# Issuing the value weighings of two neighbouring key tiles together in a four-batch attention kernel

## What is computed

```python
qkv = (x @ Wqkv.T + bqkv).reshape(Bb, Ss, 3, H, HD).transpose(2, 0, 3, 1, 4)
q, k, v = (qkv[0], qkv[1], qkv[2])
attn = jax.nn.softmax(jnp.einsum('bhid,bhjd->bhij', q, k) / jnp.sqrt(jnp.float32(HD)), axis=-1)
...
mod = attn * coh[..., None]
mod = mod / (mod.sum(-1, keepdims=True) + 1e-08)
...
mod = (1.0 - fi) * mod + fi * fa[:, None, :, None]
out = jnp.einsum('bhij,bhjd->bhid', mod, v).transpose(0, 2, 1, 3).reshape(Bb, Ss, Ee)
return out @ Wout.T + bout
```

## Time and profile before

| | |
|---|---|
| three runs | 308.05, 307.35, 306.35 us (median 307.35) |
| profiled execution, span from the first to the last instruction | 302.4 us |
| TensorE (PE) busy | 272.4 us, 90% |
| VectorE (DVE) busy | 197.7 us, 65% |
| ScalarE (ACT) busy | 176.2 us, 58% |
| GpSimd (POOL) busy | 157.9 us, 52% |
| mean granted TensorE clock | 0.977 |

### The profile page before, as it was taken

How to read it: one execution, slowest core, us unless ns; L and a number is a source line. 1 busy time by engine, 2 the same in 40 slices (tenths; PEclk the granted TensorE clock), 3 DMA queues, 4 the chain that set the end, 5 groups by cost and what they waited for, 6 DMA issues and landing times.

```text
span 302.4 us, 4278 instructions
## 1 busy us (share of the span) xinstructions
PE 272.4 (90%) x1579; PEld 130.0 (43%) x1579; DVE 197.7 (65%) x227; ACT 176.2 (58%) x214; POOL 157.9 (52%) x143
## 2 busy tenths in 40 slices
PE   8999397598979999999899999999999988899973
PEld 6447244233534444444444454446444433344422
DVE  6485355556777677887577668785876778864113
ACT  3224034456667768676448677674667666655760
POOL 3933639998199999993003069960000399900000
PEclk9999687989999999999999999999999999999999
DMA  7717839739773934399318933695159500101002
GB/s 240 214 44 217 192 53 121 175 61 120 138 245 52 125 37 152 98 117 173 126 69 109 109 83 122 96 121 171 54 86 121 90 2 4 33 3 69 1 0 72
DMA packets 16020, 31.11 MB, mean 103 GB/s; under 512 B 2232, under 2 KB 8248, under 8 KB 14656
## 3 DMA queue, kind: packets, MB, share of 16 engines
q1 hardware_dynamic: 15168, 30.15, 50.9%
q10 hardware_dynamic: 832, 0.69, 0.8%
HBM read 20.21 MB, written 10.49 MB: 102 GB/s over the span
## 4 chain that ended last, share of the span: by engine, by line
PE 59%; DVE 18%; DMA 13%; issue 4%; SPq 2%; POOL 1%; ACT 1%; DVEq 0%; ACTq 0%; POOLq 0%
PE o_ps L1018 15%; DVE maxima L660 14%; PE job_ps L794 12%; PE pair_ps L990 11%; PE pair_ps L1003 9%; DMA stack<-qk_scratch 6%; PE job_ps L908 4%; DMA stack<-max_rows 3%; DVE qk_lo L676 2%; DMA w_raw<-wqkvT 2%; DMA qk_scratch<-qk_lo 2%; SPq L313 1%; PE pair_ps L882 1%; PE job_ps L849 1%; PE pair_ps L794 1%
## 5 line engine op out<-in xcount | busy, mean ns | idle before, releaser
L660 DVE TENSOR_REDUCE maxima<-pair_ps 128x2 f32<-128x1024 f32 x128 | 155.5, 1222 | 69.1 <-PE pair_ps L990 69.1
L513 ACT ACTIVATE probs<-pair_ps 128x1024 f32<-128x1024 f32 x128 | 130.8, 1025 | 65.6 <-PE pair_ps L1003 64.9
L990 PE MATMUL pair_ps<-stack 48*128 48x512 f32 x256 | 64.5, 500 | 8.2 <-DMA stack<-qk_scratch 7.6
L1018 PE MATMUL o_ps<-probs,vals 128*32 128x512 f32 x512 | 69.0, 612 | 0.8 <-ACT probs L513 0.8
L1003 PE MATMUL pair_ps<-stack 49*128 49x512 f32 x256 | 57.1, 444 | 9.8 <-DVE maxima L660 7.0
L990 PEld LDWEIGHTS pair_ps<-stack 48*128 48x128 f32 x256 | 24.2, 186 | 56.9 <-issue 40.0
L389 POOL TENSOR_TENSOR vals<-v_new,row 128x256 f32<-128x256 f32 x16 | 11.3, 733 | 48.5 <-ACT v_new L545 48.2
L1003 PEld LDWEIGHTS pair_ps<-stack 49*128 49x128 f32 x256 | 24.4, 187 | 28.3 <-DVE maxima L660 18.8
L488 POOL TENSOR_TENSOR prod<-amap,x_tok 128x1024 f32<-128x1024 f32 x12 | 28.6, 2382 | 0.9
L372 POOL TENSOR_TENSOR x_lo<-x_raw,x_hi 128x1024 fp32r<-128x1024 f32 x3 | 7.1, 2375 | 32.9 <-ACT x_hi L519 32.8
L490 POOL TENSOR_TENSOR y<-y,prod 128x1024 f32<-128x1024 f32 x8 | 19.1, 2382 | 0.6
(11 more groups left out here) (134 smaller groups left out, 297.2 us busy)
## 6 DMA issues: line engine op xcount, KB each, us to landing
stack<-qk_scratch SPq DMA_DIRECT2D x42, 256.0 KB, 8.9
qk_scratch<-qk_hi SPq DMA_DIRECT2D x16, 256.0 KB, 5.4
qk_scratch<-qk_lo SPq DMA_DIRECT2D x16, 256.0 KB, 5.8
x_tok<-x SPq DMA_DIRECT2D x4, 512.0 KB, 14.3
out<-y SPq DMA_DIRECT2D x8, 256.0 KB, 2.2
x_raw<-xT SPq DMA_DIRECT2D x3, 512.0 KB, 5.9
fa_now<-fa_rows SPq DMA_DIRECT2D x4, 256.0 KB, 7.7
stack<-qk_scratch SPq DMA_DIRECT2D x6, 128.0 KB, 4.7
```

The costliest lines, as they stand in the source:

```text
L513: nc.scalar.activation(probs[:, t % 4, :, :], ps[:, :, :], ACT.Exp, scale=SCALE).then_inc(exp_done, 1)
L660: nc.vector.tensor_reduce(maxima[:, gg % 2, :, pair, i], pair_ps[SLOT["S", u]][:, :, :], AX_X, ALU.max, negate=True).then_inc(s_reduced, 1)
L990: ins = nc.tensor.matmul(pair_ps[SLOT["S", u]][:, a, :], stack[64 * a:64 * a + ROWS, 0, p, i * P:(i + 1) * P], stack[64 * a:64 * a + ROWS, ...
L1018: ins = nc.tensor.matmul(o_ps[h * VW:(h + 1) * VW, :], vals[:, j, gg % G * HG + h, :], probs[:, (2 * k + h // 2) % 4, h % 2, :], start=(j ...
```

## The change

Tiles 2m and 2m + 1 are both weighed in step 4m + 17. The odd tile stays where it was; the even one moves two steps later, behind the S and T of two more steps and the job of the even step between. The ring of `probs` grows from four to six tiles, and ACT's wait on `av_done` is loosened by one tile to match. To make room, `w_dir` becomes another name for `oT`, and `dir_part` another name for the memory of `o_tok`; both are only used at the very start.

```diff
-def weigh_at(n):
-
-    k, odd = divmod(n - LEAD - 3, 2)
-    return k if not odd and 0 <= k < STEPS // 2 else None
+RING = 6
+
+
+def weighed_at(n):
+
+    m, rest = divmod(n - LEAD - 5, 4)
+    return (2 * m, 2 * m + 1) if rest == 0 and 0 <= m < STEPS // 4 else ()
...
-        w_dir = sb("w_dir", [P, KT, 512])
...
-        dir_part = sb("dir_part", [P, 2, S], F32R)
...
-        probs = sb("probs", [P, 4, 2, S])
+        probs = sb("probs", [P, RING, 2, S])
...
+        w_dir = oT
+        dir_part = o_tok[:, :, :].rearrange("p i e -> p (i e)").rearrange("p (n s) -> p n s", n=2).bitcast(F32R)
...
-                    wait(act, av_done, t // 2 - 1)
+                    wait(act, av_done, t // 2 - RING // 2 + 1)
                 ps = pair_ps[SLOT["T", t]]
-                nc.scalar.activation(probs[:, t % 4, :, :], ps[:, :, :], ACT.Exp, scale=SCALE).then_inc(exp_done, 1)
+                nc.scalar.activation(probs[:, t % RING, :, :], ps[:, :, :], ACT.Exp, scale=SCALE).then_inc(exp_done, 1)
...
-                k = weigh_at(n)
-                if k is not None and k % IT == IT - 1 and k // IT != G * B - 2:
-                    attention_out(k // IT)
+                for k in weighed_at(n):
+                    if k % IT == IT - 1 and k // IT != G * B - 2:
+                        attention_out(k // IT)
...
-                                           probs[:, (2 * k + h // 2) % 4, h % 2, :], start=(j == 0), stop=(j == IT - 1))
+                                           probs[:, (2 * k + h // 2) % RING, h % 2, :], start=(j == 0), stop=(j == IT - 1))
...
-                k = weigh_at(n)
-                if k is not None:
+                for k in weighed_at(n):
                     weigh_values(k)
```

More of the change, by code:

```diff
@@ L775, in _ @@
                     qk_low(("q0", 0))
-                k = weigh_at(n)
-                if k is not None and k % IT == IT - 1 and k // IT == G * B - 2:
-                    attention_out(k // IT)
+                for k in weighed_at(n):
+                    if k % IT == IT - 1 and k // IT == G * B - 2:
+                        attention_out(k // IT)
                 for job in JOBS.get(n - 1, []):
```

## The result

The changed kernel takes 330.52 us (median) where the kernel before takes 307.48 us: 7.5% slower, ratio 1.0746 with a 95% interval of 1.0717 to 1.0775. The forecast was 319.3 us and the range ended at 324. The direction was right, the size about half. The four executions took 329.63, 330.43, 330.62 and 472.84 us; the last, at a clock of 1.0, is outside the ratio, has no trace and stays unexplained. The profiled span grew from 302.4 to 328.4 us, by 26.0 us.

The account below looks back on a forecast made before the run. TensorE was taken as the bound, DVE close behind in places. Batches two and three 8.0, first 1.3, last 0.5, start 1.3, end 0.9 sum to +12.0 us: span 302.4 to 314.4, median 319.3 us, range 309.5 to 324.

Parts of the forecast that it names:

- What bounds the kernel: Whole kernel: TensorE is the bound, busy 90%, with DVE close behind in places, where T waits for a reduction.
- the walk of a block: Block of four steps: T(48) waits for reduce(47), second weighing exposed, +0.87 us; S(50) at 6.12 instead of 5.25.
- the sum: All added costs: second and third batch 8.0, first 1.3, last 0.5, start 1.3, end 0.9; together 12.0 us.
- its 0.1 a block: Each block of a full batch: estimated 0.1 us gained as a pair lets DVE catch up; 4.8 became 4.0 a batch.
- the saving: TensorE's own time: W's end and costlier changes to S and T fall away, 0.32 us a pair, 10.2 us without waits.
- The fast rival: T in steps 0 modulo 4 finds its reduction ready, every pair keeps its 0.32 us: 298 us; chance 0.11.
- half a weighing in step 17: First pair's second weighing may run at 1.2 GHz, costing another 0.87 us or nothing; half was taken.
- the clock falls: Pair at half clock in the first batch, or idle time lowering the clock later: 325 to 330 us; chance 0.06.
- The start: W of tile 0 moves behind the 2.57 us stack transfer wait: 0.87 us; with the half-clock allowance, 1.3 together.
- The end: Before T(132), a W that lay inside the 2.40 us transfer of the maxima now stands outside: 0.9 us.

Follow-up runs that it names:

- the filled kernel: Changed kernel, pairs kept, with S repeated in T's waits and idle products in the transfer waits and the two end waits; 321.88 us, ratio 1.060.
- two filled runs: Changed kernel with S repeated where T waits for the reduction, 324.46 us; the same plus idle products in the transfer and end waits, 321.88 us.
- the kernel with fewer pairs: Changed kernel with pairs for tiles 4 to 55 only (26 pairs), the other tiles weighed singly at their old steps, nothing filled; 327.0 us, ratio 1.069.

## Why the prediction was half right

**What bounds the kernel, and the walk of a block: right.** T(24) came 1.82 us behind S(23) and S(26) at 6.10, walked 6.12. The second weighing costs 0.85, taken 0.87. The eleven middle groups cost 8.4 us at full clock, against 8.5 in the sum, and this is no luck of the total: in the filled kernel the four groups of the third batch (the groups of eight steps between two mileposts) are 0.6, 1.2, 1.5 and 0.8 us longer than before, where the walk, with its 0.1 a block off, had 0.3, 1.2, 1.5 and 1.0. The second batch came to 3.4 against 4.0, the three groups of the last to 0.8 against 0.5. (One reading was off: the low clock slices of the earlier trace rows are 5 to 7 and 9, not 5 to 8. Nothing hangs on it.) The mechanism is the one forecast: a weighing hid beside DVE's reduction, and idle time has taken its place, while the saving, of which the block shows T to S at 0.24 us, is too small against it. The fast rival, that only the changes of tiling count, is out: T waits just where it had to be free.

**The clock: wrong, and the step that failed.** The sum had 0.4 us for it, half a weighing in step 17. In the rivals I gave "the clock falls" a chance of 0.06, with 325 to 330 us, and argued that "waits of 0.85 us repeat in the last batch at a clock of 1.0". That row is true of the kernel before and says nothing of one with waits in more places; with pairs in that very batch the clock fell there. The measured 330.5 us stands at the upper end of that rival. The filled kernels give its price. In the middle groups 184.0 - 178.5 = 5.5 us; a group with a fall is 1.4 to 3.3 us longer than the same group filled. In the first three, 60.1 against 57.5 and 56.2 in the two filled runs, 2.6 to 3.9 us, and 0.9 more in the pair of step 17, which none of the two healed: half clock cost it 1.7 us, and had cost the W there 0.9 before already. At the end 43.9 - 39.3 - 2.4 = 2.2 us. In all 11.2 to 12.5 us of the 26, with the same number of instructions. The growth of TensorE's busy time, 12.4 us, says the same by another way. Before, half clock took 0.023 x 2 x 302.4 = 14 us of the span; after, 0.078 x 2 x 328.4 = 51 us.

**The start: right in structure.** W of tile 0 was exposed, as said, and both weighings of step 17 ran at half clock, where I had counted the second as half likely. TensorE's timeline after, beside the earlier trace rows:

```profile
57.92 0.50 PE L993 MATMUL pair_ps<-stack 48*128 48x512 f32 x2 [2.14 <-DMA stack<-qk_scratch]
...
59.75 0.79 PE L1006 MATMUL pair_ps<-stack 49*128 49x512 f32 x2 [0.42 <-DVE maxima L663]
60.47 3.64 PE L1021 MATMUL o_ps<-probs,vals 128*32 128x512 f32 x16
64.04 0.38 PE L852 MATMUL job_ps<-ident,maxima 128*16 128x128 f32 x1
```

The pair takes 3.57 us; the W of the kernel before took 1.87.

**The end: mis-sized.** The sum had 0.9 us, and it measured 2.4. TensorE's timeline after, from T(127) and T(128) on:

```profile
297.16 0.64 PE L1006 MATMUL pair_ps<-stack 49*128 49x512 f32 x4
299.25 0.66 PE L869 MATMUL job_ps<-ident,o_raw 128*128 128x128 f32 x4 [1.44 <-DVE y L735]
...
302.11 0.28 PE L852 MATMUL job_ps<-ident,maxima 128*16 128x128 f32 x1
...
304.52 0.60 PE L1006 MATMUL pair_ps<-stack 49*128 49x512 f32 x2 [1.46 <-DMA stack<-max_rows]
```

I had seen the wait for the maxima's transfer, which grew from 0.46 to 1.46 us. I had missed the one ahead of the transposes in step 128, on DVE's reading of the output product: 1.44 us, where the weighing of step 127 used to stand. Before, 0.26 us of it were open:

```profile
276.54 0.66 PE L866 MATMUL job_ps<-ident,o_raw 128*128 128x128 f32 x4 [0.26 <-DVE y L732]
```

Two weighings covered two waits there, and both were taken out; the pair ahead of the maxima adds its own 0.85.

**The sum.** Structure: 8.4 in the middle, 1.8 to 3.1 in the first three groups (2.2 in the sum, 1.3 for the first batch and 0.9 for the start), 2.4 at the end: 12.6 to 13.9 us against the forecast's 11.6. Clock: 11.2 to 12.5 against 0.4. The 0.9 us ahead of the first transposes stay unexplained and are within what profiles differ by there.

**What stays open.** That idle time lets the clock fall is shown by both directions: filled, it holds (full speed from the 10th slice on in the kernel with everything filled); with waits added and no pair, it falls (0.833). Which waits do it, and how often, is not: the same block ran at full clock in step 25 and had its pair at half in step 57, and the kernel with fewer pairs, in its one trace, had more falls among the same 22.

## What to carry to other kernels

Work of TensorE that has no deadline is worth most where TensorE would otherwise wait; taking it from there to save a change of tiling moved 0.87 us into the open for 0.3 us saved. Where an edit adds idle time to a TensorE that is nearly always busy, the clock is a term of the sum, here nearly as large as all the others together, and its absence in the trace of before is no evidence. The cheap test is to fill the waits with idle products into a buffer that is free: it separates structure from clock, and sometimes is itself the faster kernel.

## What was not expected of the hardware

TensorE's clock fell to 1.2 GHz in the middle of a kernel whose TensorE was busy 87% of the span, and where none of TensorE's waits for DVE in that stretch was longer than 0.94 us. The Trainium skill, TensorE: Matmul & The Clock Gate (HAM oscillation — how this bites in real kernels), tells of a kernel that falls back at each DMA wait of 3 to 5 us; the waits here, 0.84 us at T(24) among them, are much shorter. The section behind it (A second HAM failure mode: psum-queue depth-cycling) describes a second kind, idle times between groups of products frequent enough for the clock to go to and fro. This trace agrees in that, with slow pairs at 132, 142, 151 and 220 us and full clock between them; whether it is the same cause no run here shows. And 40 products that compute nothing made the kernel before 1.0% faster (0.4 to 1.6%).
